# Attention with a bank of its own for the spread inverse sums, three score banks, and transposes cut in two

## The reference

```python
x = x + xattn(ctx_1024, layernorm(x), mask, ...)
x = x + ffn(layernorm(x), centroids, expert_biases, Ws_up, Ws_down, W_up, W_down)

# xattn(x, latents): 16 heads of 64; keys and values over [xn; ln], 512 of them
q = ln @ Wq; k, v = split(concat([xn, ln], 1) @ Wkv)
attn = softmax(mask(q * 64**-0.5 @ k.T))
out = layer_norm((attn @ v) @ Wout)
# ffn: sigmoid gates of the 8 best of 64 experts, silu between W_up and W_down, plus a shared expert
```

## Time and profile before

| | |
|---|---|
| median of 3 runs | 476.85 us |
| the profiled execution | 475.22 us |
| its span, first to last instruction | 473.2 us |
| granted TensorE clock, mean | 0.959 |
| PE busy | 364.5 us, 77% |
| DVE busy | 270.1 us, 57% |
| ACT busy | 274.9 us, 58% |
| POOL busy | 268.3 us, 57% |
| transposes | 128, a median of 3.2 us from issue to landing |

### The profile page before, as it was taken

One profiled execution on the slowest core, in us unless ns is written; L12 is line 12 of the kernel. 1 busy time (PEld: TensorE's weight loads), 2 busy tenths in 40 slices (PEclk: granted clock), 3 DMA queues, 4 the chain that ended last, 5 costly groups with the idle time before them and its releaser, 6 DMA issues.

```text
span 473.2 us, 7526 instructions
## 1 busy us (share of the span) xinstructions
PE 364.5 (77%) x2225; PEld 266.9 (56%) x2225; DVE 270.1 (57%) x700; ACT 274.9 (58%) x539; POOL 268.3 (57%) x345
## 2 busy tenths in 40 slices
PE   3679768777678677776786776795338999999996
PEld 2558445555556555555565555573226677777774
DVE  2889755435345354354453453562387877777885
ACT  3777964564654645646546556476046766666681
POOL 3120427577576675675765766777122377776782
PEclk9999998999999999999999999998556999999999
DMA  8100227966969876977868767779400000000001
GB/s 234 44 1 1 44 44 134 175 109 123 174 113 130 160 130 116 162 128 135 155 123 143 146 127 132 156 131 192 101 1 0 2 0 0 0 0 0 1 0 45
DMA packets 154914, 42.77 MB, mean 90 GB/s; under 512 B 144768, under 2 KB 154496, under 8 KB 154880
## 3 DMA queue, kind: packets, MB, share of 16 engines
q1 hardware_dynamic: 154448, 40.78, 46.6%
q10 hardware_dynamic: 432, 1.57, 1.0%
HBM read 8.26 MB, written 0.52 MB: 19 GB/s over the span
## 4 chain that ended last, share of the span: by engine, by line
PE 54%; issue 16%; ACT 12%; DVE 8%; DMA 5%; POOL 3%; DVEq 0%; SPq 0%; ACTq 0%; POOLq 0%
PE ps L709 15%; PE ps L711 13%; PE ps L710 13%; PE ps L819 4%; PE ps L828 4%; ACT prob L543 3%; DMA pT<-p 3%; PE ps L939 3%; ACT rinv_sb L558 3%; POOL p L388 2%; DMA tok<-in_ctx 2%; DVE v L1195 2%; ACT v L571 1%; ACT p L551 1%; ACT sel L619 1%
## 5 line engine op out<-in xcount | busy, mean ns | idle before, releaser
L388 POOL TENSOR_TENSOR p<-prob,p 128x512 f16<-128x512 f32 x128 | 147.4, 1162 | 114.2 <-ACT p L551 114.2
L543 ACT ACTIVATE prob<-sc,p_bias 128x512 f32<-128x512 f32 x128 | 91.2, 712 | 116.0 <-DVE p_bias L1166 116.0
L1157 DVE CUSTOM_DVE_ANT_0 sc<-ps,mask_add 128x512 f32<-128x512 f32 x128 | 85.7, 687 | 21.9 <-PE ps L711 21.7
L1187 DVE TENSOR_TENSOR q_lo<-ps,q_hi 128x512 fp32r<-128x512 f32 x32 | 22.1, 690 | 112.8 <-ACT q_hi L563 112.8
L709 PE MATMUL ps<-kv_hi,q_hi 128*128 128x512 f32 x128 | 56.8, 443 | 0.0
L804 PE MATMUL ps<-pT,v 128*64 128x256 f16 x768 | 49.6, 280 | 7.0 <-DMA pT<-p 7.0
L804 PEld LDWEIGHTS ps<-pT,v 128*64 128x64 f16 x768 | 40.7, 112 | 19.3 <-issue 19.2
L711 PE MATMUL ps<-kv_hi,q_lo 128*128 128x512 f32 x128 | 50.8, 397 | 0.0
L710 PE MATMUL ps<-kv_lo,q_hi 128*128 128x512 f32 x128 | 50.4, 394 | 0.0
L1344 DVE TENSOR_TENSOR h<-h,ps 128x1024 f32<-128x1024 f32 (+1 forms) x32 | 39.1, 1221 | 18.9 <-PE ps L939 17.6
L709 PE MATMUL ps<-kv_hi,w_all 128*128 128x512 f32 x32 | 14.6, 456 | 38.4 <-ACT rinv_sb L558 38.4
(11 more groups left out here) (192 smaller groups left out, 755.4 us busy)
## 6 DMA issues: line engine op xcount, KB each, us to landing
pT<-p SPq DMA_TRANSPOSE x128, 3.2
wup_s<-in_L_ffn_W_up SPq DMA_DIRECT2D x8, 256.0 KB, 3.4
wdn_s<-in_L_ffn_W_down SPq DMA_DIRECT2D x8, 256.0 KB, 3.8
wkv_s<-in_L_xattn_Wkv ACTq DMA_DIRECT2D x2, 512.0 KB, 6.9
x_in<-in_x SPq DMA_DIRECT2D x2, 256.0 KB, 7.9
wq_s<-in_L_xattn_Wq ACTq DMA_DIRECT2D x1, 512.0 KB, 7.4
tok<-in_ctx SPq DMA_DIRECT2D x4, 128.0 KB, 8.0
wo_s<-in_L_xattn_Wout SPq DMA_DIRECT2D x1, 512.0 KB, 5.2
```

The costliest lines, as they stand in the source:

```text
L388: pool.tensor_tensor(p16[:, t, 1, :], prob[:, t, :], p16[:, t, 0, :], ALU.subtract).then_inc(s_plo, 1)
L543: act.activation(prob[:, t, :], sc[:, t, :], ACT.Exp, bias=p_bias[:, t:t + 1], scale=-1.0, accum_out=p_sum[:, i % 2, t:t + 1]).then_inc(s_ ...
L1157: return dve.tensor_tensor_reduce(sc[:, t, :], ps[:, SCORE_BANK + t, :], mask_add[:, i % B, :], -SCALE, -LEAST, ALU.add, ALU.min, neg_max[ ...
```

## The change

- PSUM: the spread inverse sums get bank 5 for themselves (`INV_BANK`); bank 7 keeps the queries. Scores use three banks, 2 to 4, in rotation over all tiles, so a score waits for the mask three tiles before it.
- The inverse's copy moves from ACT to DVE, to the head of `normalise_out`, without its scale; the scale is put once on the output weights `wo_s` by POOL, before the attention.
- DVE's order in iteration i becomes masks 0 and 1, copy and normalising of step i-3, shift, masks 2 and 3, the inversion, shift, the low part of the queries.
- PE's order becomes all four scores, projection of step i-3, spreading and attending of step i-2, queries. The two waits over bank 7 go.
- SP issues a transposing DMA for the high part (128 x 512) as soon as that is there and another for the low part: high 0, high 1, low 0, low 1, high 2, high 3, low 2, low 3. `s_turned` counts 32 a step. The wait for the attending two steps back stands before high 0.

```diff
-        OUT_BANK, SCORE_BANK, AV_BANK, Q_BANK = 0, 2, 6, 7
+        OUT_BANK, SCORE_BANK, INV_BANK, AV_BANK, Q_BANK = 0, 2, 5, 6, 7
+        SCORE_BANKS = 3
...
-            def turn_p(i, t):
-
-                sp.wait_ge(s_plo, i * TILES + t + 1)
+            def turn_high(i, t):
+
+                if t < 2:
+                    sp.wait_ge(s_phi_act, i * 2 + t + 1)
+                else:
+                    sp.wait_ge(s_phi_pool, i * 2 + t - 1)
                 if t == 0 and i >= 2:
                     sp.wait_ge(s_av, i - 1)
-                sp.dma_start_transpose(pT[:, i % 2, t // QT, :, t % QT, :],
-                                       p16[:, t, :, :].rearrange("p a k -> p (a k)")).then_inc(s_turned[t], 16)
+                sp.dma_start_transpose(pT[:, i % 2, t // QT, 0:KT, t % QT, :], p16[:, t, 0, :]).then_inc(s_turned[t], 16)
+
+            def turn_low(i, t):
+
+                sp.wait_ge(s_plo, i * TILES + t + 1)
+                sp.dma_start_transpose(pT[:, i % 2, t // QT, KT:2 * KT, t % QT, :], p16[:, t, 1, :])\
+                    .then_inc(s_turned[t], 16)
 
             for i in range(STEPS):
-                for t in range(TILES):
-                    turn_p(i, t)
+                turn_high(i, 0)
+                turn_high(i, 1)
+                turn_low(i, 0)
+                turn_low(i, 1)
+                turn_high(i, 2)
+                turn_high(i, 3)
+                turn_low(i, 2)
+                turn_low(i, 3)
...
+            pool.wait_ge(s_wo, 16)
+            pool.wait_ge(s_range, 3)
+            pool.tensor_scalar(wo_s[:, :, :], wo_s[:, :, :], range_v[:, 7:8], None, ALU.mult).then_inc(s_woscaled, 1)
...
-            def take_inverse(i):
-
-                act.wait_ge(s_rb, i + 1)
-                if i:
-                    act.wait_ge(s_ao, i)
-                act.activation(rinv_sb[:, :], ps[:, Q_BANK, 0:S], ACT.Copy, scale=range_v[:, 7:8]).then_inc(s_rbsb, 1)
...
+                three(ps[:, SCORE_BANK + (i * TILES + t) % SCORE_BANKS, :], q_hi[:, head, at:at + P], q_lo[:, head, at:at + P],
                       kv_hi[:, b, :], kv_lo[:, b, :]).then_inc(s_score, 1)
...
             def spread_inverse(i):
 
                 pe.wait_ge(s_rinv, i + 1)
-                pe.wait_ge(s_qlo, min(i + 5, STEPS))
                 if i:
                     pe.wait_ge(s_rbsb, i)
...
-                pe.wait_ge(s_masked, (i - 1) * TILES + t + 1)
-                scores(i % B, t)
+                pe.wait_ge(s_masked, i * TILES + t + 1 - SCORE_BANKS)
+                scores(i, t)
 
             for i in range(1, STEPS + 2):
                 if i < STEPS:
-                    score_step(i, 0)
-                    score_step(i, 1)
+                    for t in range(TILES):
+                        score_step(i, t)
+                if i >= 3:
+                    project(i - 3)
                 if i >= 2:
                     spread_inverse(i - 2)
-                if i >= 3:
-                    project(i - 3)
-                if i < STEPS:
-                    score_step(i, 2)
-                    score_step(i, 3)
-                if i >= 2:
                     attend(i - 2)
                 if i <= STEPS - B:
                     pe.wait_ge(s_qlo, i + 3)
-                    if i >= 2:
-                        pe.wait_ge(s_rbsb, i - 1)
                     queries((i + 3) // B, (i - 1) % B)
...
             def normalise_out(i):
 
+                dve.wait_ge(s_rb, i + 1)
+                if i:
+                    dve.wait_ge(s_ao, i)
+                dve.tensor_copy(rinv_sb[:, :], ps[:, INV_BANK, 0:S]).then_inc(s_rbsb, 1)
                 dve.wait_ge(s_av, i + 1)
...
             for i in range(1, STEPS):
                 mask_scores(i, 0)
                 mask_scores(i, 1)
+                if i >= 3:
+                    normalise_out(i - 3)
+                shift_range(i, 0)
+                mask_scores(i, 2)
+                mask_scores(i, 3)
                 invert(i - 1)
-                mask_scores(i, 2)
-                shift_range(i, 0)
-                mask_scores(i, 3)
                 shift_range(i, 2)
                 if i <= STEPS - B:
                     q_low(i + 3, (i - 1) % B)
-                if i >= 2:
-                    normalise_out(i - 2)
+            normalise_out(STEPS - 3)
             invert(STEPS - 1)
             normalise_out(STEPS - 2)
```

More of the change, by code:

```diff
@@ L247, in xattn_moe @@
         s_phi_act, s_phi_pool, s_plo = sem("s_phi_act"), sem("s_phi_pool"), sem("s_plo")
-        s_av, s_rb, s_rbsb, s_ao, s_wout = sem("s_av"), sem("s_rb"), sem("s_rbsb"), sem("s_ao"), sem("s_wout")
+        s_av, s_rb, s_rbsb, s_ao, s_wout, s_woscaled = (sem("s_av"), sem("s_rb"), sem("s_rbsb"), sem("s_ao"), sem("s_wout"),
+                                                       sem("s_woscaled"))
         s_q, s_qhi, s_qlo = sem("s_q"), sem("s_qhi"), sem("s_qlo")
@@ L378, in split_high @@
                 if i:
-                    pool.wait_ge(s_turned[t], 16 * i)
+                    pool.wait_ge(s_turned[t], 32 * i)
                 pool.tensor_copy(p16[:, t, 0, :], prob[:, t, :]).then_inc(s_phi_pool, 1)
@@ L549, in split_high @@
                 if i:
-                    act.wait_ge(s_turned[t], 16 * i)
+                    act.wait_ge(s_turned[t], 32 * i)
                 act.activation(p16[:, t, 0, :], prob[:, t, :], ACT.Copy).then_inc(s_phi_act, 1)
-            def take_inverse(i):
-                act.wait_ge(s_rb, i + 1)
-                if i:
-                    act.wait_ge(s_ao, i)
-                act.activation(rinv_sb[:, :], ps[:, Q_BANK, 0:S], ACT.Copy, scale=range_v[:, 7:8]).then_inc(s_rbsb, 1)
             def q_high(c, quarter, bank=Q_BANK):
@@ L599, in _ @@
                 split_high(i, 0)
-                if i >= 2:
-                    take_inverse(i - 2)
                 exp(i, 2)
@@ L757, in queries, with scores @@
                       kv_hi[:, rows, S:2 * S], kv_lo[:, rows, S:2 * S]).then_inc(s_q, 1)
-            def scores(b, t):
+            def scores(i, t):
+                b = i % B
                 head, qt = t // QT, t % QT
                 at = b * S + qt * P
-                three(ps[:, SCORE_BANK + t, :], q_hi[:, head, at:at + P], q_lo[:, head, at:at + P],
+                three(ps[:, SCORE_BANK + (i * TILES + t) % SCORE_BANKS, :], q_hi[:, head, at:at + P], q_lo[:, head, at:at + P],
                       kv_hi[:, b, :], kv_lo[:, b, :]).then_inc(s_score, 1)
@@ L790, in _ @@
                         pe.wait_ge(s_qlo, 4)
+                    if n >= SCORE_BANKS:
+                        pe.wait_ge(s_masked, n + 1 - SCORE_BANKS)
                     scores(0, n)
@@ L796, in attend @@
                 for t in range(TILES):
-                    pe.wait_ge(s_turned[t], 16 * (i + 1))
+                    pe.wait_ge(s_turned[t], 32 * (i + 1))
                 if i:
@@ L818, in spread_inverse @@
                         t = head * QT + qt
-                        mm = pe.matmul(ps[head * DH:(head + 1) * DH, Q_BANK, qt * P:(qt + 1) * P],
+                        mm = pe.matmul(ps[head * DH:(head + 1) * DH, INV_BANK, qt * P:(qt + 1) * P],
                                        p_rinv[:, i % 2, t:t + 1].broadcast_to([P, DH]), ident[:, :],
@@ L833, in turn_out @@
                 pe.wait_ge(s_outT, half + 1)
-                if half == 0:
-                    pe.wait_ge(s_rbsb, STEPS)
                 for j in range(4):
@@ L841, in _ @@
             pe.wait_ge(s_vlo, CHUNKS)
-            pe.wait_ge(s_wo, 16)
+            pe.wait_ge(s_woscaled, 1)
             for n in range(2):
@@ L881, in _ @@
             pe.transpose(ps[:, AV_BANK, 0:E], cent[:, :], ident[0:E, 0:E]).then_inc(s_cent, 1)
-            turn_out(1, SCORE_BANK + 3)
+            turn_out(1, INV_BANK)
             def turn_input(half):
@@ L1156, in mask_scores @@
                 dve.sem_inc(s_held, 1)
-                return dve.tensor_tensor_reduce(sc[:, t, :], ps[:, SCORE_BANK + t, :],
+                return dve.tensor_tensor_reduce(sc[:, t, :], ps[:, SCORE_BANK + (i * TILES + t) % SCORE_BANKS, :],
                                                 mask_add[:, i % B, :], -SCALE, -LEAST, ALU.add, ALU.min,
@@ L1214, in _ @@
                     shift_range(0, n)
-            turned = [[ps[:, bank, j * P:(j + 1) * P] for j in range(4)] for bank in (Q_BANK, SCORE_BANK + 3)]
+            turned = [[ps[:, bank, j * P:(j + 1) * P] for j in range(4)] for bank in (Q_BANK, INV_BANK)]
             def variances(n):
```

2 lines of the change are left out of this document (removed).

## The result

The changed kernel takes **557.91 us** (median of 4 runs, 557.39 to 558.03), beside 476.71 for the kernel before in the same session (475.48 to 478.0). The ratio is **1.170, 95% interval 1.167 to 1.173: slower**. The forecast was 471 with a range of 438 to 500, so the result lies well outside it. What came true is the rival that had got the smallest chance, 0.08: the issue of a transpose does not shrink with its columns. It had given 550.

A forecast was written before the change was run, and what follows sets the result against it. SP's queue of transposes was to bound the step at 8.23 us instead of 8.66: 27 steps -11.6, tail +7.1, landing -1.1, copy +0.45, together -5.2 on 475.22, so 470.0, written as 471 for the median; range 438 to 500.

The forecast's parts named there:

- the rival that had got the smallest chance, 0.08: Transposes on SP: the issue does not shrink at all, 10.79 us a step, 550 us in all; chance 0.08.
- The transfers: SP's eight half transposes a step: 0.85 us an issue, bounds 0.62 and 1.23; 0.91 when directly following.
- the surcharge for following directly: SP's queue: 0.06 us added to an issue that directly follows another, bounds 0 and 0.10.
- break-even of 0.93: Issue length on SP, in us, from which 27 steps and tail together come to zero; above it, slower.
- the queue's sum: SP's time a step: 7.64 for eight transposes, 0.33 weight loads, 0.26 long issues; 8.23 us.
- The tail by the prediction's own formula: Attending matmuls of step 27 to the last step: 4 x (7.64 + 0.26) + 1.31 = 32.9 us, +7.1.
- SP's queue becomes the bound: Attention steps: SP's issuing needs 8.23 us, over the DVE loop's 7.30 and just below today's 8.66.
- The DMA engines carry the same bytes: Transfers of a step: 5.6 us for transposes plus some 0.7 for weights, 6.3, still under 8.23.
- The loop of 7.30: New wait loop through ACT and DVE without PE's leg: 7.30 us a step, 7.2 to 7.4 over the copy's bounds.
- shift to exponential 0.20: Last term of the DVE loop, from the first shift to the next exponential: 0.20 us.
- The copy on DVE: Copy of the inverse sums ahead of the normalising: 0.41 us, between 0.33 and 0.45.
- What was put at nothing: Three score banks, reversed spread and project with later inverting, POOL's scaling of output weights: all hidden, 0 us.

## Why the prediction was wrong, and where it was right

**The step that failed** is the one headed "The transfers": "I take a fixed 0.47 and halve the rest: 0.85". The truth lay next to its upper bound of 1.23: the shortest issue of 512 columns took 1.19, and with the surcharge for following directly 1.264, against 0.91. The fixed part was taken from plain copies, which hold SP for 0.47 to 0.64; a transpose's fixed part is another one. The issues by size as the traces of the runs have them, the shortest one and the median of those that directly follow another:

| columns x partitions | shortest | directly following |
|---|---|---|
| 256 x 128 | 1.17 | 1.25 |
| 512 x 128 | 1.19 | 1.26 |
| 1024 x 64 | 1.19 | 1.27 |
| 1024 x 128 | 1.23 | 1.33 to 1.34 |
| 2048 x 128 | 1.32 | not clear |

The shortest ones of 128 partitions (1.167, 1.188, 1.231, 1.316) lie on a line, an estimate from these four: about 1.15 fixed and 0.011 for each block of 128 x 128. The tile of 64 partitions, with as many elements as four such blocks, took 1.193 and fits it.

The rival with 0.08 came true, but not for the reason written beside it: it argued that the number of rows on the partitions stays, and the run with 64 partitions shows that this number is not the reason. That its 550 lies so near was luck as far as that argument goes. Nothing in the rows excluded the upper bound, though, since the kernel before had only one size of transpose and so nothing that told columns from a fixed part. The chance of 0.08 and a range that left this case out were the error in judgement. The break-even of 0.93, or 0.87 without the surcharge, lies four tenths of the way from 0.62 to 1.23, so more than half of what the bounds allowed was slower; the prediction gave that 0.37.

**The rest of the queue's sum held.** 8 x (1.264 + 0.045) is 10.47, with 0.33 for the weight loads 10.80; the step of 11.06 leaves 0.26 for long issues, the figure forecast. The surcharge for following directly, forecast at 0.06, was 0.05 to 0.08. The tail by the prediction's own formula, 4 x (10.47 + 0.26) + 1.31, is 44.2, measured 42.79. With the measured issue the prediction's sum gives 27 x (11.06 - 8.66) + 18.4 on 475.2, less 0.65: 557.7, and the profiled execution took 558.0.

**That SP's queue becomes the bound** was right, and so were the signs named for it: SP without gaps, POOL's casts and ACT's high parts waiting for landings, the queries no longer waiting for ACT. "Issues above 0.93 and steps above 8.7" had been named as what would show the forecast wrong, and that is what the trace holds.

**"The DMA engines carry the same bytes"** and stay under the queue: right (0.56 and 0.71 busy). The landing after the issue, forecast about 1.1 shorter than 3.21, got only 0.7 shorter, 2.5 at the median:

```profile
pT<-p SPq DMA_TRANSPOSE x256, 2.5
```

The Trainium skill says, in "DMA: Bandwidth & Descriptors", section "Issuing engines are not separate DMA queues", that starting a DMA is usually short beside the DMA itself. The trace of the changed kernel says the opposite for these: 1.26 of issue beside 0.7 to 0.9 of transfer.

**The bank and the copy.** The loop of 7.30 was never seen in the changed kernel, since the queue covered it, but the runs with four whole transposes show it: 7.36 once the shift is out of POOL's way. In its forecast form one term was mis-sized: "shift to exponential 0.20", from the earlier trace rows, held where POOL stood idle beside it; in its new place it was 0.75 in the step shown (238.24 to 238.99), and 22 of the 32 first shifts were held up. The copy on DVE was forecast at 0.41 and took 0.42, but the normalising began 0.52 after the copy (204.68 to 205.20), where 0.45 had been summed; no row showed the 0.04 that the prediction put between them. This is the 0.06 from 7.30 to 7.36.

**What was put at nothing shows no cost.** Three score banks, the reversed order and POOL's scaling of the weights: the kernel with all of them and four transposes reached the summed loop but for 0.06, and the kernel with none of them and eight halves took the same time as the change. None of the three was tried by itself.

So the change holds a gain and a loss: without its halves it is 455, and with the shift moved ahead and done by a reduction 435, 8.5% under the kernel before. With its halves all of that is hidden.

## What to carry to other kernels

Count the transposes on a queue, not only their bytes: an issue of 1.2 us hardly depends on its size here, and a cut that starts a transfer earlier doubles it. The bytes decide nothing while the queue is the fuller of the two; with the queue relieved, the DMA engines were 0.95 busy. When one cost has bounds that lie on both sides of the break-even and no row speaks for the middle, both bounds belong in the range. And a tiny instruction on the critical chain is priced by what runs beside it on the other engine, not by its size: take its longest case, not its median.

## What the runs showed of the hardware

**A transpose's issue is almost all fixed.** 1.17 to 1.32 us on SP (the shortest) from 256 to 2048 columns, beside 0.47 to 0.64 for a plain copy. What SP does in it, no view shows.

**VectorE's small shift waits for GpSimd.** In the kernel with four whole transposes the `tensor_scalar` on two columns took between 0.16 and 0.95 us: 0.72 where POOL's subtraction was running, ending 0.03 behind it, 0.17 where POOL was not subtracting. A `tensor_reduce` on four columns in the same place took 0.15. The Trainium skill says so in "SBUF — State Buffer", section "Who interferes with whom": `tensor_scalar` can enter the two-port mode, in which VectorE and GpSimd take a shared pair of ports as an exclusive lock, and `tensor_reduce` never contends on trn2. The traces agree in both halves, with 0.72 and 0.15. In the changed kernel the queue covered it, as far as the traces show; that was not tried by itself:

```profile
L1169 DVE TENSOR_SCALAR p_bias<-neg_max x64: 157/170/1111, 47.9 to 390.2; 128x2 f32<-128x2 f32 x64
```

Its median is short, its mean over the attention stage 0.50. Which shift is held depends on where POOL stands: in the changed kernel 26 of the 32 second shifts of a step took more than 0.3 us and 2 of the first ones, in the kernel with four whole transposes 22 of the first and 2 of the second.

**TensorE's clock fell with the queue.** The granted clock was 1.00 in the step of the earlier trace rows and 0.84 in the first of the two stretches after, that is partly at the level of 1.2 GHz; in the tail it was 0.66 (0.89 before). Ahead of it PE had stood waiting for masks and landings. With four whole transposes and the reduction it is back at 1.00 (80 to 260 us). It seems to have cost little, since SP's queue went on without a pause above 0.10 in the tail; this was not tried by itself. The last attending matmuls wait 6.15 for the landing (the view's window ends after 14 of the 24; all 24 take 2.77 here, at the lower level, and 2.77 in the kernel before as well).

```profile
415.70 1.71 PE L816 MATMUL ps<-pT,v 128*64 128x256 f16 x14 [6.15 <-DMA pT<-p]
```
